# Graph attention over 32 batches on one core: the input turned by DMA, both output halves in one bank, the maxima raised on VectorE, and the last batch written out by hand

## The reference

```python
h = jnp.maximum(_layernorm(x, axis=-1), 0.0)
q = _heads(h @ Wq + bq); k = _heads(h @ Wk + bk); v = _heads(h @ Wv + bv)
scores = jnp.einsum('bhqd,bhkd->bhqk', q, k) / np.sqrt(HEAD_SIZE)
bias = jnp.where(graph_mask, 0.0, NEG)[:, None]
probs = jax.nn.softmax(scores + bias, axis=-1)
ctx = jnp.einsum('bhqk,bhkd->bhqd', probs, v)
out = x + (merge_heads(ctx) @ Wf + bf)
```

## Time and profile before

| | |
|---|---|
| median of three runs | 616.36 us (616.36 to 617.8) |
| the profiled execution | 617.89 us, its span from first to last instruction 616.0 us |
| busy in the span: TensorE, ScalarE, GpSimd, VectorE | 97%, 84%, 81%, 74% |
| DMA engines, mean busy share of the main queue | 66.1% |
| clock granted to TensorE | 0.989 of full speed on the mean |

### The profile page before, as it was taken

How to read it: one execution, slowest core, us unless ns; L and a number is a source line. 1 busy time by engine, 2 the same in 40 slices (tenths; PEclk the granted TensorE clock), 3 DMA queues, 4 the chain that set the end, 5 groups by cost and what they waited for, 6 DMA issues and landing times.

```text
span 616.0 us, 18008 instructions
## 1 busy us (share of the span) xinstructions
PE 596.3 (97%) x6806; PEld 451.9 (73%) x6806; DVE 456.9 (74%) x1479; ACT 516.5 (84%) x1166; POOL 496.1 (81%) x529
## 2 busy tenths in 40 slices
PE   7998999999999999999999999999999999999975
PEld 7666777777777777777777777777777777777753
DVE  5878777878777777877777787777778777776762
ACT  2688888889888889988888898888889888888980
POOL 2789888888888888888888888888888888888750
PEclk9998999999999999999999999999999999999997
DMA  8056766867766786666578767666886666765573
GB/s 264 6 100 117 133 124 128 157 128 146 139 139 122 129 159 127 145 131 150 118 129 159 130 141 134 142 123 129 159 136 136 140 141 121 126 133 112 100 136 80
DMA packets 232280, 81.14 MB, mean 132 GB/s; under 512 B 214273, under 2 KB 232194, under 8 KB 232194
## 3 DMA queue, kind: packets, MB, share of 16 engines
q1 hardware_dynamic: 230992, 79.99, 66.1%
q10 hardware_dynamic: 1202, 0.01, 0.1%
HBM read 17.05 MB, written 12.58 MB: 48 GB/s over the span
## 4 chain that ended last, share of the span: by engine, by line
PE 87%; ACT 6%; DVE 2%; DMA 2%; issue 1%; POOL 1%; ACTq 0%; DVEq 0%; POOLq 0%
PE ring L858 19%; PE ring L860 19%; PE ring L859 19%; PE scores L922 11%; PE ctx L939 5%; PE ring L951 4%; PE ctx L940 3%; PE ctx L941 3%; PE ring L874 3%; ACT probs L479 2%; DMA bf_row<-in_L_gnn_bf_dram 1%; ACT qk L496 1%; ACT p_rows L484 1%; DMA p_cols<-p_rows 1%; PE ring L981 1%
## 5 line engine op out<-in xcount | busy, mean ns | idle before, releaser
L379 POOL TENSOR_TENSOR p_rows<-probs,p_rows 128x512 f16<-128x512 f32 x192 | 222.4, 1158 | 58.5 <-ACT p_rows L484 57.3
L632 DVE CUSTOM_DVE_ANT_0 logits<-scores,mask,logit_unscale 128x256 f32<-128x256 f32 x384 | 169.1, 477 | 39.0 <-PE scores L922 37.1
L479 ACT ACTIVATE probs<-logits,raised 128x256 f32<-128x256 f32 x384 | 174.3, 500 | 6.2
L858 PE MATMUL ring<-h_hi,w_hi 128*128 128x256 f16 x576 | 157.7, 274 | 0.6 <-DVE h_lo L640 0.6
L860 PE MATMUL ring<-h_hi,w_lo 128*128 128x256 f16 x576 | 157.5, 273 | 0.0
L859 PE MATMUL ring<-h_lo,w_hi 128*128 128x256 f16 x576 | 157.4, 273 | 0.0
L365 POOL TENSOR_TENSOR split<-qk,split 128x512 f16<-128x512 f32 x96 | 111.0, 1157 | 25.2 <-DVE split L648 25.2
L484 ACT ACTIVATE p_rows<-probs 128x512 f16<-128x512 f32 x192 | 121.0, 630 | 6.1
L496 ACT ACTIVATE qk<-ring,qk_bias_s,qkv_ratio 128x256 f32<-128x256 f32 x192 | 96.3, 551 | 3.9 <-PE ring L860 3.9
L939 PE MATMUL ctx<-v_hi,p_cols 128*128 128x65 f16 x768 | 90.7, 196 | 7.4 <-DMA p_cols<-p_rows 4.4
L939 PEld LDWEIGHTS ctx<-v_hi,p_cols 128*128 128x128 f16 x768 | 70.2, 97 | 33.4 <-issue 23.6
(11 more groups left out here) (89 smaller groups left out, 1222.2 us busy)
## 6 DMA issues: line engine op xcount, KB each, us to landing
x_in<-in_x_dram SPq DMA_DIRECT2D x32, 384.0 KB, 3.9
out_dram<-result SPq DMA_DIRECT2D x64, 192.0 KB, 2.2
p_cols<-p_rows SPq DMA_TRANSPOSE x192, 3.1
adj_in<-in_adj_dram SPq DMA_DIRECT2D x32, 64.0 KB, 2.6
w_raw<-in_L_gnn_Wq_dram SPq DMA_DIRECT2D x1, 576.0 KB, 5.8
w_raw<-in_L_gnn_Wv_dram SPq DMA_DIRECT2D x1, 576.0 KB, 7.9
w_raw<-in_L_gnn_Wf_dram SPq DMA_DIRECT2D x1, 576.0 KB, 9.1
w_raw<-in_L_gnn_Wk_dram SPq DMA_DIRECT2D x1, 384.0 KB, 6.8
```

Source lines behind the costliest of these rows:

```text
L379: pool.tensor_tensor(p_rows[u][:, 1], probs[u % 3][:], p_rows[u][:, 0], ALU.subtract).then_inc(p_lo_ready, 1)
L479: act.activation(probs[u % 3][:, a], logits[u % 3][:, a], ACT.Exp, bias=raised[u % 3][:, a:a + 1], scale=-1.0).then_inc(probs_ready, 1)
L632: dve.tensor_tensor_reduce(out=logits[u % 3][:, a], in0=score_bank[a][:, u % 2 * S:(u % 2 + 1) * S], in1=mask[b.parity][:, t], scale=logit ...
L858: pe.matmul(out_ap, a_hi, m_hi, start=first, stop=False)
```

## The change

The input of batches 2 to 31 is no longer turned by TensorE. ScalarE (`h_hi_rows`) and VectorE (`h_lo_rows`) split `normed` as it lies, into `h_rows`, and SP turns hi and lo together by one DMA transpose of 12 blocks into `h_cols`, two batches ahead. Both output halves use `ring[1]`. VectorE adds the constant to `least` itself, by two instructions of one column each, behind a wait for its own maxima. `v_lo_part(b, 0)` moves from the end of a cycle to behind the second unit. The cycles end at 30, and the last batch is written out: its units 4 and 5 are turned by TensorE from float32 instead of by GpSimd and DMA, and the second half of its output goes in two pieces.

```diff
+        h_rows = sb("h_rows", [P, 2, C, QT, P], F16)
+        h_cols = [sb(f"h_cols{p}", [P, 2, C, S], F16) for p in range(2)]
-        R_OUT = [ring[1], ring[3]]
+        def out_of(b, t):
+            return ring[3] if t == 1 and b.k >= B - 2 else ring[1]
+        BY_PE = 2
         def cycles(cycle):
-            for k in range(1, B + 2):
+            for k in range(1, B - 1):
...
+            def transpose_h(b):
+                wait(sp, h_lo_ready, b.count(2, 2))
+                sp.dma_start_transpose(h_cols[b.parity][:].rearrange("p w c (t k) -> p (w c t) k", k=P),
+                                       h_rows[:].rearrange("p w c t n -> p (w c t n)")).then_inc(h_placed, 16)
...
                 if here:
                     transpose_probs(b, 1)
+                if (b + 2).exists():
+                    transpose_h(b + 2)
                 if here:
                     transpose_probs(b, 2)
...
-                wait(pool, ht_ready, b.count(2, 0))
+                wait(pool, ht_ready if b.k <= BY_PE else h_lo_ready, b.count(2, 0))
...
-                wait(act, logits_ready, b.count(2 * UNITS, 2 * u + 2))
-                act.activation(raised[u % 3][:], least[u % 3][:], ACT.Identity,
-                               bias=p_raise[:, 0:1]).then_inc(raised_ready, 1)
-                wait(act, raised_ready, b.count(UNITS, u + 1))
+                wait(act, raised_ready, b.count(2 * UNITS, 2 * u + 2))
...
+            def h_hi_rows(b):
+                wait(act, h_placed, (b.k - BY_PE) * 16)
+                for t in range(QT):
+                    wait(act, norm_ready, b.count(2, t + 1))
+                    act.activation(h_rows[:, 0, :, t], normed[:, t].rearrange("p (c n) -> p c n", n=P),
+                                   ACT.Relu).then_inc(h_hi_ready, 1)
...
-                if front:
-                    h_hi_part(b + 1)
...
                 if front:
                     qk_full(b + 1, 0)
+                if (b + 2).exists():
+                    h_hi_rows(b + 2)
...
                         op0=ALU.add, op1=ALU.min, accum_out=least[u % 3][:, a:a + 1]).then_inc(logits_ready, 1)
+                dve.wait_ge(logits_ready, b.count(2 * UNITS, 2 * u + 2))
+                for a in range(2):
+                    dve.tensor_scalar(raised[u % 3][:, a:a + 1], least[u % 3][:, a:a + 1], P_RAISE, None,
+                                      ALU.add).then_inc(raised_ready, 1)
...
+            def h_lo_rows(b):
+                for t in range(QT):
+                    wait(dve, h_hi_ready, b.count(2, t + 1))
+                    dve.scalar_tensor_tensor(
+                        out=h_rows[:, 1, :, t], in0=normed[:, t].rearrange("p (c n) -> p c n", n=P),
+                        scalar=0.0, in1=h_rows[:, 0, :, t], op0=ALU.max, op1=ALU.subtract).then_inc(h_lo_ready, 1)
...
-                if j == 0:
+                if j == 0 and b.k < BY_PE:
                     wait(pe, h_lo_ready, b.count(2, 2))
+                elif j == 0:
+                    wait(pe, h_placed, (b.k - BY_PE + 1) * 16)
...
-                if t == 1 and (b + 2).exists():
-                    wait(pe, v_lo_ready, (b + 2).count(2, 1))
+                if t == 1 and b.k < B - 2:
+                    wait(pe, result_ready, b.count(2, 1))
...
                 attend(0)
-                if front:
-                    transpose_h(b + 1)
                 if (b + -2).exists():
                     project_out(b + -2, 1)
...
+            def turned_hi(u, nth):
+                act.wait_ge(pt_ready, nth)
+                act.activation(p_cols[u][:, 0].rearrange("p a s q -> p (a s q)"), last_pt[u][:],
+                               ACT.Copy).then_inc(pt_hi_ready, 1)
+            def turn_probs(u):
...
+                    for n in range(QT):
+                        o = (a * QT + n) * P
+                        mm = pe.transpose(last_pt[u][:, o:o + P], probs[u % 3][:, a, n * P:(n + 1) * P], ident[:])
```

More of the change, by code:

```diff
@@ L336, in _, with store_last @@
             transpose_probs(Batch(0), 3)
+            transpose_h(Batch(2))
             cycles(cycle)
+            def store_last(t):
+                sp.wait_ge(result_ready, LAST.count(2, t + 1))
+                sp.dma_start(out_v[LAST.k, t], normed[:, t]).then_inc(out_stored[t], 16)
+            transpose_probs(PREV, 4)
+            store(PREV + -1, 0)
+            transpose_probs(PREV, 5)
+            transpose_probs(LAST, 0)
+            store(PREV + -1, 1)
+            for u in (1, 2, 3):
+                transpose_probs(LAST, u)
+            store(PREV, 0)
+            store(PREV, 1)
+            store_last(0)
+            store_last(1)
             for t in range(QT):
@@ L676, in finish @@
                 wait(dve, out_stored[t], b.count(16, 16))
[L677 removed]
+                dve.scalar_tensor_tensor(out=result[t][:], in0=out_of(b, t)[:, 0:H], scalar=out_unscale[:, 0:1],
                                          in1=residual[b.slot][:, t], op0=ALU.mult,
@@ new lines, in _ @@
+            mask_and_max(LAST, 0)
+            mask_and_max(LAST, 1)
+            divide(PREV, 0)
+            finish(PREV + -1, 1)
+            v_lo_part(LAST, 0)
+            v_lo_part(LAST, 1)
+            mask_and_max(LAST, 2)
+            mask_and_max(LAST, 3)
+            context_lo(PREV, 0)
+            mask_and_max(LAST, 4)
+            mask_and_max(LAST, 5)
+            divide(PREV, 1)
+            finish(PREV, 0)
+            turned_lo(4, 1)
+            context_lo(PREV, 1)
+            divide(LAST, 0)
@@ L854, in _ @@
+            turned_lo(5, 2)
+            finish(PREV, 1)
+            divide_last(UP_TO, 5, 2)
+            context_lo(LAST, 0)
+            context_lo_last(UP_TO, 2)
+            divide_last(FROM, 6, 3)
+            context_lo_last(FROM, 3)
+            finish_last(0)
+            finish_last(1)
         @block.tensor
@@ new lines, in transpose_context_last, with project_out_last @@
+            def transpose_context_last(chunks, nth):
+                pe.wait_ge(context_ready, LAST.count(2, nth))
+                for c in range(chunks.start, chunks.stop):
+                    mm = pe.transpose(R_CT[1][:, c * P:(c + 1) * P],
+                                      context[1][:, 2 * c:2 * c + 2].rearrange("p h d -> p (h d)"), ident[:])
+                mm.then_inc(ct_ready, 1)
+            def project_out_last(chunks, nth):
+                pe.wait_ge(ct_lo_ready, LAST.count(2, nth))
+                pe.wait_ge(result_ready, PREV.count(2, 2))
+                for c in range(chunks.start, chunks.stop):
+                    mm = three(out_of(LAST, 1)[:, 0:H], ct_hi[1][:, c], ct_lo[1][:, c],
+                               w_hi[:, 3, c], w_lo[:, 3, c], c == 0, c == C - 1)
+                if chunks.stop == C:
+                    mm.then_inc(out_ready, 1)
```

158 lines of the change are left out of this document (125 added, 33 removed).

## The result

The changed kernel takes **629.57 us** (median of 4 runs, 627.75 to 630.55) where the kernel before takes 616.36 beside it: a ratio of 1.0208, with a 95% interval of 1.0183 to 1.0234. It is slower, and lies above the range that I gave (594 to 627). The profiled execution has a span of 628.1 us against 616.0.

A forecast was written before the change was run, and what follows sets the result against it. TensorE, busy for 97% of the span, was taken as the bound. Terms -20.7 + 6.6 + 3.0 - 4.0 = -15.1 us took the profiled 617.89 to 602.8, or 601.3 us as median; range 594 to 627.

The forecast's parts named there:

- The transposes: TensorE's six transposes of h leave 30 cycles, 0.69 us each: -20.7 us, a cycle of 17.93 becoming 17.24.
- The stall at unit 3: TensorE waits for VectorE's context, delayed by the raise: 0.22 us a cycle (0 to 0.38), 6.6 us back.
- The pair: VectorE's two h_rows instructions with two SBUF inputs, waiting for GpSimd: 0.10 us a cycle (0 to 0.65), 3.0 us.
- The spare time: Between unit 3's maxima, done at 309.6, and the third scores at 310.04: 0.4 us to spare, no stall.
- Rival (b): GpSimd's p_rows gets between the pair; third scores stall 0.45, division 0.2: cycle 18.1 to 18.6, 617 to 632 us; chance 0.30.
- (a): Rival: VectorE and GpSimd set the round, 17.7 us a cycle, 605.5 us, still faster; chance 0.24.
- (c): Rival: TensorE loses the transposes but stands as long for VectorE, stalls of 0.5 to 0.7 us, 616; chance 0.10.
- The DMA: One 12-block transpose of h joins each cycle, some 4.7 us, made a cycle early; hidden, even landing 3 us later.
- the shared bank: Output half 1 now waits for finish of half 0, which VectorE runs a cycle earlier: costs nothing.
- v_lo: Moved behind the second unit, some 4 us of VectorE work for 5 us of time: nothing, up to 0.1 us a cycle if later.
- The closing: Last batch's units 4 and 5 turned by TensorE instead of GpSimd and DMA: 4.0 us gained, between 1.5 and 6.
- The start-up: Stretch before the steady cycles: -1 to +1 us, taken as 0.

The follow-up runs named there:

- moved_behind: Changed kernel with the h_rows pair behind the division after unit 3's maxima, and the raise of units 0 and 3 behind the division following their maxima: 596.73 us.
- moved_behind_sp: moved_behind with SyncE's transpose of h put behind that of unit 2's probabilities instead of ahead: 596.38 us.
- pool_wait: Changed kernel plus one wait: GpSimd starts p_rows of unit 2 only when both h_rows instructions of VectorE are done: 600.75 us.
- psum_pair: Changed kernel with the first operand of VectorE's h_rows pair read from a PSUM bank instead of normed, leaving out the residue of h: 600.18 us.
- one_pair: Changed kernel with VectorE's two h_rows instructions made one of 768 columns: 600.50 us.
- moved_pair: Changed kernel with the h_rows pair moved from before unit 3's maxima to behind the division that follows them: 600.08 us.
- raise2_dve: Changed kernel with all raises back on ScalarE except that of unit 2, which stays on VectorE: 593.93 us.

## Why the prediction was wrong, point by point

**The transposes (17.93 to 17.24):** right. The best cycles of moved_behind and moved_behind_sp are 17.26 us.

**The stall at unit 3 (0.22, 0 to 0.38):** right in place and nearly in size: 0.27 in the changed kernel, gone when the raise stands behind the division. The raise itself costs nearly what was reckoned (0.27): without it the next instruction starts with the reading of the second maximum, and here the reading is at 313.18 and the cast behind the raise at 313.42, 0.24 later.

**The pair (0.10, bounds 0 and 0.65):** the step that failed, in its value and its upper bound. It costs about 1.0 us a cycle (18.52 against 17.50 to 17.55 where it runs through): 30 us in place of 3. The text said of this term that "the first end is nearer, as the spare time is four times what I add". The spare time was a smaller error: it was put at 0.4 us, and in pool_wait unit 3's maxima are read at 303.28 and the third scores start at 303.55, so some 0.2 us are to spare (the changed kernel's pair is 0.97 longer, and its third scores come 0.75 late). The error that decided was the time at which GpSimd asks. I took it from `p_rows` at 308.78 in the kernel before, held that against the pair's end, and found it close, "some 0.1 to 0.3 us". But the same change takes the raise away from ScalarE, and I dismissed that as a gain to an engine "which is not late anywhere". These are ScalarE's lines at unit 2 in the kernel before:

```profile
306.80 0.30 ACT L475 ACTIVATE raised<-least,p_raise 128x2 f32<-128x2 f32 x1
307.13 0.91 ACT L479 ACTIVATE probs<-logits,raised 128x256 f32<-128x256 f32 x2
308.07 0.63 ACT L484 ACTIVATE p_rows<-probs 128x512 f16<-128x512 f32 x1
```

Without the first, the other two come 0.33 us earlier, and GpSimd's request, behind 308.07 + 0.63, as much earlier, just when the raise makes VectorE later. I had moved VectorE's list by the raise and left ScalarE's where it was. Both shifts point the same way, and together they settle what I had left as a matter of chance: with unit 2's raise alone back on ScalarE (raise2_act), ScalarE is done 0.30 us after `split` instead of 0.03 before it.

**Rival (b):** right in mechanism, stated in advance with its condition, and given 0.30. Its stalls of 0.45 and 0.2 us measured 0.75 and 0.28, which together are the 1.0 us of the pair; its cycle of "18.1 to 18.6" is 18.52, and its range of 617 to 632 holds the time, which my own range, cut at 627, did not. The Trainium skill says on the page "SBUF — State Buffer", section "Who interferes with whom", that of a VectorE instruction with two SBUF inputs and a GpSimd instruction that reads SBUF the later one blocks until the first has ended. This agrees with psum_pair (1.01 us with one input in PSUM, 2.70 with both in SBUF). The lock is held for an instruction, not for a pair; that is what one_pair shows.

**Rivals (a) and (c):** (a) fell: with the pair free, TensorE is busy for 437.46 of 440 us and no other engine sets the round. (c) fell: what took the place of the 0.69 us was 1.30, and 0.27 where the pair runs through.

**The DMA, the shared bank, `v_lo`:** right. The transpose of h lands after 4.3 us (4.7 estimated), and no wait for it is seen in the steady cycles; no wait for the shared bank either. That `p_cols` becomes late once TensorE is down at 17.26 I had not looked for: the "7 us" that I counted for unit 2, which should have borne a landing 3 us later, were used up by an issue 2.4 us late and a landing 5.0 us after it.

**The closing (-4.0):** right: -3.7. Four lines of it, to be laid against the 16, 19, 22 and 22.9 us that I followed from 602.41:

```profile
615.78 0.69 DVE L955 TENSOR_TENSOR p_cols<-ring,p_cols 128x512 f16<-128x512 f32 x1 [1.64 <-ACT p_cols L670]
...
621.85 0.29 DVE L966 TENSOR_TENSOR context<-ctx,inv_sum 128x128 f32<-128x128 f32 x1
...
624.79 0.33 PE L1019 MATMUL ring<-w_hi,ct_lo 128*128 128x384 f16 x1
...
625.16 0.62 DVE L982 SCALAR_TENSOR_TENSOR normed<-ring,out_unscale,residual 128x384 f32<-128x384 f32 x1 [0.23 <-PE ring L1019]
```

They end 14.1, 19.7, 22.7 and 23.4 us after it. The wait of 2.98 us for `p_cols` is gone. How much of the 3.7 us that is was not measured, since TensorE's clock differs too: by the clocks granted in the windows I estimate some 6.8 us at the lower of its two levels (1.2 GHz, half of full speed) in the closing before (2 x 0.26 x 12.30 and 2 x 0.01 x 17.90) and some 3.5 us here (2 x 0.12 x 14.42), where it fell after TensorE had been busy for 3.6 of 6 us (604 to 610). A matmul of 384 columns at the end takes 0.33 us instead of 0.50.

**The start-up (0, -1 to +1):** the 1.6 us by which the first scores come earlier in this execution lie outside, but moved_pair, with the same start, has 0.2; so I count it as spread between executions, not as a gain.

**The sum.** With the pair's term at 1.0 us a cycle in place of 0.10, my sum gives 601.3 + 27 = 628.3, against 629.57; and where the pair runs through, 600.1 to 600.8 against the forecast of 601.3 (a cycle of 17.50 to 17.55 against 17.56). The change with its raise left on ScalarE (raise_act) runs in 593.57 us, 3.6% faster than the kernel before, the fastest seen here beside raise2_dve.

## What to carry to other kernels

Where two engines exclude each other, ask for each edit who asks first afterwards, and move every engine's list by that edit, the one that gets faster too: an engine that is "not late anywhere" still sets when its reader asks. Two short locking instructions in a row are two chances for the other engine; one of twice the length, a place where the other engine waits for VectorE anyway, or a wait that puts the other engine behind, each gave back 29 us here.

An edit is not free because it is free beside one consumer: the raise had room ahead of `context` in the kernel before, and cost 14 us through `h_lo`, the instruction behind it.

## What the runs showed of the hardware

Between two VectorE instructions that read two SBUF inputs and follow each other directly, a GpSimd instruction that is already waiting goes first. The nine kernels in which the pair is two instructions, reads SBUF alone and has no written wait between (the changed one among them) have 270 such pairs. In 41 of them a GpSimd instruction starts 0.20 to 0.46 us before the second of the pair, and that one takes 1.35 to 1.51 us; in the other 229, where GpSimd starts after it (from 0.04 us on) or not at all, it takes 0.54 to 0.55. In the first pair of psum_pair GpSimd starts 0.46 us ahead as well, and the second takes 0.55: with one input in PSUM nothing stands. The instruction that loses is shown as running in the trace (`p_rows` 1.39, 1.51 and 1.55 us against 1.16 undisturbed; the pair 2.70 against 1.01), so such a wait appears as a longer duration and not as idle time. The page's group of the pair in the changed kernel (busy and mean ns of one, then idle time before) shows 1372 ns and no idle time:

```profile
L740 DVE SCALAR_TENSOR_TENSOR h_rows<-normed,h_rows 128x384 f16<-128x384 f32 x60 | 80.0, 1372 | 0.0
```
